# A selective-scan and ternary-MLP kernel: two Softplus results by ScalarE, a shorter chain for h's scales, and four more products by C on VectorE

## What is computed

```python
# first block: x = x + tanh(g_xattn) * mamba(ctx, layernorm(x))
u  = silu(conv4(in_proj @ ctx) + conv_b)            # 512 channels x 512 steps
dt_low, B, C = split(x_proj @ u, [16, 32])          # rank 16, state 16
dt = softplus(dt_proj @ dt_low + dt_proj_b)
state = state * exp(dt * A) + (dt * u) * B          # over time, for each channel and state
y  = sum_n(state * C) + D * u
y  = y * silu(z)
# second block: x = x + tanh(g_ffn) * ffn(layernorm(x))
h   = silu(bitlinear(x, w1)) * bitlinear(x, w2)     # 2048 wide
out = bitlinear(h, w3)
def bitlinear(x, w):                                # xq: 8 bits by row, wq in {-1, 0, 1}
    xn = rmsnorm(x)
    s = 127 / max(max|xn|, 1e-5)                    # the scale of a row
    return (round(xn * s) / s) @ ternary(w).T
```

## Time and profile before

| | before |
|---|---|
| median of three runs | 653.24 us |
| the profiled execution, its own time | 650.76 us |
| its span, first to last instruction | 648.6 us |
| busy DVE, POOL, ACT, PE | 583.1, 582.5, 506.6, 488.0 us |

### The profile page before, as it was taken

One profiled execution on the slowest core, in us unless ns is written; L12 is line 12 of the kernel. 1 busy time (PEld: TensorE's weight loads), 2 busy tenths in 40 slices (PEclk: granted clock), 3 DMA queues, 4 the chain that ended last, 5 costly groups with the idle time before them and its releaser, 6 DMA issues.

```text
span 648.6 us, 7576 instructions
## 1 busy us (share of the span) xinstructions
PE 488.0 (75%) x2396; PEld 283.1 (44%) x2396; DVE 583.1 (90%) x695; ACT 506.6 (78%) x946; POOL 582.5 (90%) x324
## 2 busy tenths in 40 slices
PE   9797888995464777687665668787686776678987
PEld 3253444543353444444443435354353543335543
DVE  7779779999999899999999999999998999999665
ACT  6854757688999787787698797888899897886675
POOL 1499999997999999999999999999999999999431
PEclk9898989997655989999895978789898998979999
DMA  5698587569960101149830110118931011110001
GB/s 187 212 405 297 186 314 284 206 246 389 401 267 0 34 7 33 33 156 222 271 99 6 33 32 18 32 57 242 334 98 26 24 34 32 18 42 24 1 16 50
DMA packets 49815, 87.04 MB, mean 134 GB/s; under 512 B 27808, under 2 KB 30496, under 8 KB 46704
## 3 DMA queue, kind: packets, MB, share of 16 engines
q1 hardware_dynamic: 49776, 86.57, 40.0%
HBM read 72.53 MB, written 7.73 MB: 124 GB/s over the span
## 4 chain that ended last, share of the span: by engine, by line
DVE 27%; POOL 26%; PE 16%; issue 14%; ACT 11%; DMA 4%; SPq 1%; DVEq 0%; POOLq 0%; ACTq 0%
DVE hh L824 12%; POOL hh L729 7%; POOL hh L863 7%; POOL hh L738 6%; POOL hh L868 5%; DMA wq<-x 3%; ACT da L782 3%; DVE room L1103 3%; PE bank_y L901 2%; DVE da L824 2%; PE bank_b L265 2%; DVE sm L1151 2%; PE bank_t L277 1%; PE bank_a L1075 1%; PE bank_a L265 1%
## 5 line engine op out<-in xcount | busy, mean ns | idle before, releaser
L824 DVE TENSOR_TENSOR_SCAN hh<-da,hh 128x1024 f32<-128x1024 f32 x112 | 255.0, 2281 | 4.0 <-ACT da L789 2.5
L901 PE MATMUL bank_y<-ident,hh 128*128 128x128 f32 x1024 | 144.4, 290 | 13.4 <-POOL hh L868 7.9
L901 PEld LDWEIGHTS bank_y<-ident,hh 128*128 128x128 f32 x1024 | 127.6, 151 | 44.5 <-issue 18.9
L868 POOL TENSOR_TENSOR hh<-hh,cc 128x1024 f32<-128x1024 f32 x57 | 134.8, 2365 | 0.0
L863 POOL TENSOR_TENSOR hh<-hh,cc 128x1024 f32<-128x1024 f32 x55 | 129.5, 2355 | 0.3 <-ACT hl L814 0.3
L738 POOL TENSOR_TENSOR hh<-pair,bb 128x1024 f32<-128x1024 f32 x30 | 70.9, 2363 | 24.3 <-DMA bb<-xd_scratch 23.2
L738 POOL TENSOR_TENSOR hh<-wq,bb 128x1024 f32<-128x1024 f32 x32 | 75.5, 2367 | 4.4 <-PE bank_y L901 4.3
L729 POOL TENSOR_TENSOR hh<-pair,bb 128x1024 f32<-128x1024 f32 x32 | 75.2, 2358 | 0.8 <-PE bank_y L901 0.8
L729 POOL TENSOR_TENSOR hh<-wq,bb 128x1024 f32<-128x1024 f32 x32 | 75.3, 2353 | 0.7 <-PE bank_y L901 0.7
L789 ACT ACTIVATE da<-pair,cst 128x511 f32<-128x511 f32 x64 | 41.4, 682 | 24.8 <-DVE hh L824 24.8
L782 ACT ACTIVATE da<-wq,cst 128x255 f32<-128x255 f32 x128 | 53.4, 464 | 7.4 <-DVE hh L824 7.2
(11 more groups left out here) (289 smaller groups left out, 994.8 us busy)
## 6 DMA issues: line engine op xcount, KB each, us to landing
bb<-xd_scratch SPq DMA_DIRECT2D x32, 512.0 KB, 6.4
cc<-xd_scratch SPq DMA_DIRECT2D x32, 512.0 KB, 8.2
wq<-weights SPq DMA_DIRECT2D x12, 1024.0 KB, 6.8
stage<-weights SPq DMA_DIRECT2D x8, 1024.0 KB, 5.6
xin<-x SPq DMA_DIRECT2D x4, 1024.0 KB, 5.6
room<-weights SPq DMA_DIRECT2D x4, 1024.0 KB, 8.5
u_scratch<-wq SPq DMA_DIRECT2D x6, 512.0 KB, 3.0
wq<-x SPq DMA_DIRECT2D x2, 1024.0 KB, 18.8
```

The lines of the kernel that those rows point to most:

```text
L824: v.tensor_tensor_scan(to, da, h, 0.0, ALU.mult, ALU.add).then_inc(s_scan, 1)
L868: ins = g_.tensor_tensor(hh[k % NH][:, :, :], hh[k % NH][:, :, :], cc[:, s * GN:(s + 1) * GN, :], ALU.mult)
L901: mm = pe.matmul(bank_y[:, (first + c) * P:(first + c + 1) * P], flat(hh[k % NH])[:, at:at + P], ident[:, :], start=False, stop=(s == STEP ...
```

## The change

There are three parts.

1. **Softplus twice.** For groups 4 to 15 ACT now writes Softplus to `dt2` in SBUF and then, a second time, in place in the bank. DVE's copy goes, with its wait for ACT's old exps; DVE's product by u waits for the second Softplus. The waits of the exps and of `state_gain` for the copy go too.
2. **Scales of h**, for tiles 0 to 12. Six small DVE instructions become four (`peak_of_both`: the peak of both halves; `scale_vector`: peak times rk, not under 1e-5; its reciprocal; that times rk times 127). ACT gets two small ones: rk, the power times kk (`rk_scalar`, slot `TILE[i] + 6`), and the factor of the output (`fin_scalar`, slot `TILE[i] + 7`). POOL's power moves from slot `TILE[i] + 7` to `TILE[i] + 6`; for tile 12 from between the products of steps 125 and 126 to ahead of that of step 124.
3. **Products by C** of steps 47, 59, 87 and 118 go from POOL to DVE.

```diff
-BY_VECTOR = (14, 16, 25, 45, 49, 53, 62, 67, 68, 73, 77, 84, 90, 94, 115, 122)
+BY_VECTOR = (14, 16, 25, 45, 47, 49, 53, 59, 62, 67, 68, 73, 77, 84, 87, 90, 94, 115, 118, 122)
...
         def dt_scalar(act, g):
             act.wait_ge(*GP.of(("dt", g)))
-            ins = act.activation(dt2[g % 4] if g < NE else dt_bank(g)[:, :], dt_bank(g)[:, :], ACT.Softplus)
-            if 0 < g < NE:
+            ins = act.activation(dt2[g % 4], dt_bank(g)[:, :], ACT.Softplus)
+            if g:
                 GA.did(ins)
                 ins = act.activation(dt_bank(g)[:, :], dt_bank(g)[:, :], ACT.Softplus)
             GA.did(ins, ("dt", g))
...
                 v.wait_ge(*d_u[g // 2 % 2].of(g // 2))
-                v.wait_ge(s_exp, STEPS * (g - 3))
-                GV.did(v.tensor_copy(dt2[g % 4], dt_bank(g)[:, :]), ("copied", g))
...
+        def peak_of_both(v, i):
+            v.wait_ge(*MV.of(("peak", i, 1)))
+            MV.did(v.tensor_scalar(am1, amh[:, 0:1], amh[:, 1:2], None, ALU.max), ("am", i))
+
+        def rk_scalar(act, i):
+
+            act.wait_ge(*MG.of(("rh", i)))
+            MA.did(act.activation(rk, rh, ACT.Copy, scale=kk[:, i % NE:i % NE + 1]), ("rk", i))
+
+        def scale_vector(v, i):
+            v.wait_ge(*MV.of(("am", i)))
+            v.wait_ge(*MA.of(("rk", i)))
+            MV.did(v.tensor_scalar(hm, am1, rk, 1e-5, ALU.mult, ALU.max), ("hm", i))
+            v.wait_ge(*MV.now())
+            MV.did(v.reciprocal(hinv, hm))
+            v.wait_ge(*MV.now())
+            MV.did(v.tensor_scalar(csh, hinv, rk, 127.0, ALU.mult, ALU.mult), ("csh", i))
+
+        def fin_scalar(act, i):
+            act.wait_ge(*MV.of(("hm", i)))
+            MA.did(act.activation(fin[i % 2], hm, ACT.Copy, scale=g3d), ("fin", i))
...
                     for i in range(END):
-                        if k == tile_slot(i) + 7:
+                        if k == tile_slot(i) + 6:
                             rh_pool(g_, i)
...
                 times_c(g_, 125)
-                rh_pool(g_, 12)
                 times_c(g_, 126)
```

More of the change, by code:

```diff
@@ L121, in build @@
         dtw, xpw = sb("dtw", [P, DM]), sb("xpw", [P, NE, ROWS])
-        sm = sb("sm", [P, 282])
+        sm = sb("sm", [P, 285])
         ident16 = sb("ident16", [P, P], F16)
@@ L180, in build @@
         gates = cst[:, 92:94]
-        col = iter(range(282))
+        col = iter(range(285))
         def small(n=1):
@@ L199, in build @@
         ssq, ssv, amh = [small(3) for _ in range(3)]
-        am1, ram1, rh, rk_most, rk_am, csh = [small() for _ in range(6)]
+        am1, ram1, rh, rk, rk_most, rk_am, hm, hinv, csh = [small() for _ in range(9)]
         fin = [small() for _ in range(2)]
@@ L773, in exp @@
                     act.wait_ge(*PV.of("a_neg"))
-                if s == 0:
-                    act.wait_ge(*(GA.of(("dt", g)) if g < NE else GV.of(("copied", g))))
+                if s == 0 and g < NE:
+                    act.wait_ge(*GA.of(("dt", g)))
             if split(k):
@@ L1159, in scales_vector @@
             if part == 0:
-                v.wait_ge(*MV.of(("peak", i, NCH - 1 if at_end(i) else 1)))
-                if at_end(i):
-                    MV.did(v.tensor_scalar(am1, amh[:, 0:1], amh[:, 1:2], amh[:, 2:3], ALU.max, ALU.max))
-                else:
-                    MV.did(v.tensor_scalar(am1, amh[:, 0:1], amh[:, 1:2], None, ALU.max))
+                v.wait_ge(*MV.of(("peak", i, NCH - 1)))
+                MV.did(v.tensor_scalar(am1, amh[:, 0:1], amh[:, 1:2], amh[:, 2:3], ALU.max, ALU.max))
                 v.wait_ge(*MV.now())
@@ L1278, in out_vector @@
             v.wait_ge(*MP.of(("o", i)))
+            if not at_end(i):
+                v.wait_ge(*MA.of(("fin", i)))
             MV.did(v.scalar_tensor_tensor(out=x2_at(i), in0=bank_g(i)[:, :], scalar=fin[i % 2], in1=x2_at(i),
@@ L1599, in _ @@
                             hq_scalar(act, i, 0)
+                            fin_scalar(act, i)
                             if not by_dma(i):
                                 hq_scalar(act, i, 1)
+                        if k == tile_slot(i) + 6:
+                            rk_scalar(act, i)
                         if k == tile_slot(i) + 8 and by_dma(i):
@@ L1684, in _ @@
                 hq_scalar(act, 12, 0)
+                fin_scalar(act, 12)
                 tanh_scalar(act, 13, 1)
@@ L2019, in _ @@
                         times_c_vector(v, k + LEAD - 1)
-                scales_vector(v, 12, 1)
+                scale_vector(v, 12)
                 gated_vector(v, 13, 0)
```

9 lines of the change are left out of this document (4 added, 5 removed).

## The result

The changed kernel takes 654.88 us (median of 21 runs, 652.12 to 657.58), the kernel before 652.68 us in the same rounds (21 runs, 651.22 to 655.89). The ratio is 1.0029, with a 95% interval from 1.0018 to 1.0040: slower by 0.3%. The profiled execution took 654.85 us, its span is 652.8 us.

The account below looks back on a forecast made before the run. POOL's work sets the pace, with waits for ACT's mean square ahead of the power; S falls to -3.25 by tile 9, P ends at -1.2, so 1.2 us slower: 654.4 us against the median, range 647.5 to 658.5.

Parts of the forecast that it names:

- Tile 7, S = -1.8: S is how much earlier the chain of DVE and ACT gets; at tile 7 it was to be 1.8 us late.
- Step 87: Its product by C on DVE stands behind the peak, the exp of step 89 waits: the chain loses 2.4 us.
- Steps 47 and 59: Their products by C on DVE cost the chain of DVE and ACT 2.3 us together.
- Tiles 7 to 9, another 1.45: Between these tiles the chain of DVE and ACT loses 1.15 and 0.3 us more, reaching S = -3.25.
- the pair at slot 99: ACT's second Softplus (1.0 us) and rk (0.15) come through to DVE there: 1.15 us lost.
- the small instructions: Small ACT instructions of tiles 7 and 8 cost the chain another 0.3 us.
- Step 106 4.0 us later: POOL, held by tile 9's mean square and the power, starts step 106 4.0 us later.
- P = -1.2 behind step 118: P is how much earlier POOL gets; from -3.5, step 118's product leaving POOL gives 2.3 us back: -1.2.
- DVE's own lateness doesn't reach the last product: At the end, the last scan was 2.7 us ahead of POOL's last product, so DVE's delay would not count.
- Relief of both: Rival: DVE's list 8.6 us and POOL's 9.2 us shorter, POOL keeps it all, median 644.0 us; chance 0.06.
- DVE's chain wins on balance: Rival: same waits, but S at tile 7 is +1.5; 3.7 us faster, 649.5 us; chance 0.24.
- ScalarE becomes the bound: Rival: 1.0 us of extra Softplus reaches DVE at all six pairs, exps run late; 658 us; chance 0.20.

Follow-up runs that it names:

- e1: The changed kernel without part 3, so parts 1 and 2 alone: 653.03 us, ratio 1.0004 against the kernel before.
- e6: The changed kernel with step 87's product back on POOL and the power back in slot TILE[i] + 7 except for tile 12: 652.22 us, ratio 0.9970.
- e11: The kernel before with PE's sums ahead of the chunk's products in 39 slots, nothing else changed: 652.24 us, ratio 0.9980.
- e2: The kernel before with part 3 alone, the four products by C moved to DVE: 656.42 us, ratio 1.0057.
- e4: The changed kernel with the product of step 87 back on POOL; those of 47, 59 and 118 stay on DVE: 652.08 us, ratio 0.9992.

## Why the prediction came out

The forecast was 654.4 us, the likeliest case "slower by 1.2 us". Measured were 654.88 us and 1.9 us by the ratio. The mechanism was the one forecast, with one step wrong, two errors that cancelled, and luck in how close the number is.

- *Tile 7, S = -1.8.* Measured: the mean square ends at 456.18, so S is -0.34. Step 87 cost 2.15 us (forecast 2.4; DVE's wait for ACT behind it 1.23). Parts 1 and 2 won 3.3 us (e1), forecast 2.9. Steps 47 and 59 cost 1.1 net, forecast 2.3. A likely reading is that the term of 1.15 us for each left out that a chain which waits a little later gets part of it back. The three sum to 0.05 us won from step 30 on, and the profile shows 0.55 lost; column 40-44, where this execution has the low clock and e1 has not, accounts for it with 0.67. No term of the sum stood for the clock.
- *Tiles 7 to 9, another 1.45.* Measured 2.9: the pair at slot 99 with its rk took 1.09 of the forecast 1.15 (steps 102 to 104), the small instructions 0.24 of 0.3. A Softplus has a mean of 597 ns in the changed kernel (583 in the earlier trace rows); the 0.72 us by the Trainium skill (ScalarE: Activation LUTs, Rules for kernel authors) are not borne out. The 0.3 us in that rule of the Trainium skill are given for an activation whose bias is a column of values, and this Softplus has no such bias. Nowhere in the sum was the 1.48 us of TensorE's clock at slot 95. This error and the one at tile 7 cancel by luck: the mean square of tile 9 was forecast for 513.9 and ended at 513.94.
- *Step 106 4.0 us later.* Measured 4.28.
- *P = -1.2 behind step 118, and "DVE's own lateness doesn't reach the last product".* This step failed. POOL did get to 1.5 us late behind step 118, and then lost all of it. PE's sums of step 120 and POOL's product by B of step 126, which needs that buffer, in the changed kernel and then in the kernel before:

```profile
590.50 1.04 PE L898 MATMUL bank_y<-ident,hh 128*128 128x128 f32 x8
...
591.62 2.35 POOL L727 TENSOR_TENSOR hh<-wq,bb 128x1024 f32<-128x1024 f32 x1 [2.69 <-PE bank_y L898]
```

```profile
585.18 1.04 PE L901 MATMUL bank_y<-ident,hh 128*128 128x128 f32 x8
...
587.39 2.37 POOL L729 TENSOR_TENSOR hh<-wq,bb 128x1024 f32<-128x1024 f32 x1
```

  The sums came 5.3 us later, POOL had 1.2 us of room, and everything behind is 4.2 us later. I had looked at the last scan alone, and not at the buffers six steps back. P was forecast as -1.2 and came out as -4.2.
- *What holds POOL.* The prediction reads the 20.5 us of the earlier trace rows as a place where POOL waits in the stretch; all of it lay behind the scan. I forecast idle time before the power at most of tiles 2 to 9. It was there at 3, 6 and 7 only; the greater part stood before the products by B, waiting for sums. The sums wait in PE's queue behind matmuls that wait for DVE, so this is the chain of DVE and ACT again, and in part the order of PE. With the power in its old slot (e6) POOL's idle time in the stretch stays as large, before products by B.
- *The sum against the median.* By the profiled executions the change costs 4.1 us, by the medians about 2. In the table, twelve of the thirteen rows lose more from 30 to 127 than their ratio says, by 0.2 to 3.4 us, e11 among them. The likeliest reading is that the one profiled execution of before was a good one: 650.76 us are 1.9 under its median of 652.68, and none of its gates waits for the sums in the stretch, while the two such waits of the changed kernel cost it 2.95 us. There is no second profile of before, so this stays open. It would also be why the failed step, worth 3 us, left the number so close; by the profiled executions alone the forecast was 2.9 us short.

*The rivals.* Relief of both: the change answers it, with DVE busy for 6.5 us less, POOL for 8.7 less and the time up; so does e2 for POOL alone, with 9 us less and 0.6% more. By the Trainium skill (Perfetto Trace Analysis, Identifying the Most-Contended Engine) the engine with the highest occupancy is the one to relieve; here DVE and POOL were both relieved and the time rose, so the trace does not agree. DVE's chain wins on balance (its terms sum to an S of +2.05, not the +1.5 that the prediction states): it did without step 87 (e4, scan of step 100 1.7 us earlier than before), not with it. ScalarE becomes the bound: its second Softplus came through whole at slot 99, with 0.6 us at slot 37.
